# Four graph layers on one core: relational loops over tiles ordered by node block, second relation table and output made inside the loops

## The chip, the cores and the metric

The kernel runs on one core of one Trainium2 chip. The metric is device time in microseconds of one execution. Before the change it is 18669.26 us, the median of three runs (18641.42 to 18669.32).

## The reference, cut to what matters

Four layers over 12500 nodes and 212500 edges sorted by destination: a weighted sum over edges, a hyperbolic layer, three attention layers, and two relational layers, each added to `x`. The change rewrites the last layer:

```python
def _rgcn_conv(x, src, dst, edge_type, W_r, W_root, b):
    seg = dst * r + edge_type
    agg = segment_sum(x[src], seg).reshape(n, r, d)
    mean = agg / maximum(cnt, 1.0)
    return einsum('nrd,rdk->nk', mean, W_r) + x @ W_root + b
h = x                              # 12500 x 64
for l in range(2):                 # 65 relations, W[l] is 65 x 64 x 64
    h = relu(_rgcn_conv(h, ..., W[l], root[l], bias[l])) + relu(h @ res_W[l] + res_b[l])
```

## The kernel before, in words

Engines run their own streams and meet at counting semaphores; a `Phase` (L165) owns its buffers and semaphores and ends with a barrier of all engines. Edges stand in 1664 tiles of 128 (`ET`), in chunks of `K` = 8 tiles: 208 chunks. Nodes stand in blocks of 128.

The order of phases (L2462 to L2520) is: `prepare` (edge arrays padded, loaded and transposed), `begin` (x loaded, layer norm), `project`, `bucket_places` (a histogram loop), `edges_ordered` (edges scattered by source into a DRAM bucket of 65 MB, which `prepare` clears with 48 DMAs on ACT's queue, L285), the first two layers, three attention layers with `after_attention`, and then twice this:

- `typed_tables` (L2085): for 100 node blocks, 9 products give h times each of 65 relation matrices and of `root` and `res_W` (67 rows of 64 floats a node). PE makes them, ACT and DVE copy them out of PSUM, SP stores 2.1 MB a block to the DRAM table `typed`.
- `edges_relational` (L2190): per chunk, POOL gathers 8 x 128 rows of the table by source and relation (L2231). DVE scales them by 1/count (L2303) and makes a one-hot of the place of each edge in its tile's window (`member`, L2275). PE multiplies both (`product`, L2361), and DVE adds the 64 x 128 result into `sums`, a column per node, at a register's offset (L2320). The first relational loop also finds 1/count: SP loads 8 windows of `inv_count` a chunk (L2220), PE transposes `member` (L2343), ACT copies that out (L2255), PE multiplies it with the window (`from_dst`, L2351), DVE picks the relation (L2280, L2288, L2293).
- `columns_to_nodes` (L1625) transposes `sums`, and `after_relational` (L2382) adds the own rows and biases.

`rounds` (L128) writes each engine's order out by hand: a list of (step, lead), where turn t does the step of chunk t + lead, four turns to a loop body. Buffers have 2 or 4 slots, so a step waits for the chunk 2 or 4 before it.

## Time and profile before

| | us |
|---|---|
| median of three runs | 18669.26 |
| profiled execution, its own time | 18656.17 |
| its span | 18654.4 |
| PE, DVE, ACT, POOL busy | 12203.1, 12936.0, 7253.8, 11319.3 |

The span is cut into stages by phase. Times below are from the span's start. A row of the timeline gives start, duration, engine, line, operation with its tiles, how many are merged, and in brackets the idle time before it and what ended it. No engine is busy for more than 69% of the span, so what a stage costs is read from the wait that ends last in it.

### The profile page before, as it was taken

To read this page: it belongs to the slowest core of one execution; us is meant where nothing else is said; L and a number is where in the kernel's file an instruction comes from. 1 tells how busy PE (TensorE), PEld (TensorE's weight loads), DVE (VectorE), ACT (ScalarE), POOL (GpSimd) and SP (SyncE) were. 2 spreads that over 40 slices of the span, in tenths; PEclk is the share of its full clock that TensorE was granted. 3 is DMA by queue.
4 is the path that set the end of the run, shared out by engine and by line. 5 is a ranking of instruction groups with operands and counts; after the bars stand their busy time and mean duration, and the time that the engine had idled before them with its cause. 6 is when DMAs were issued, how large, how long until landed. Compare 5 with 4: busy or idle time off the path is not lost. (4 is left out here: it accounts for less than half of the span.)

```text
span 18654.4 us, 354278 instructions
## 1 busy us (share of the span) xinstructions
PE 12203.1 (65%) x79434; PEld 9406.9 (50%) x79435; DVE 12936.0 (69%) x30593; ACT 7253.8 (39%) x19156; POOL 11319.3 (61%) x11773
## 2 busy tenths in 40 slices
PE   3434436499996577776777767777777776843333
PEld 2322224366664466664666656665456665533332
DVE  4877768777776788887888878887555555543334
ACT  0111118455554466654666546665321111410000
POOL 0477770177774477774777657776047776057775
PEclk9999999977776565555655555565886666965555
DMA  5233334333334222223222222223752223931112
GB/s 190 69 94 94 94 86 111 93 103 102 103 102 81 59 58 58 58 54 57 58 58 58 57 54 58 58 58 62 325 188 53 53 53 59 375 118 26 26 26 47
DMA packets 1461776, 1649.61 MB, mean 88 GB/s; under 512 B 964011, under 2 KB 1068475, under 8 KB 1429565
## 3 DMA queue, kind: packets, MB, share of 16 engines
q1 hardware_dynamic: 1050273, 1054.17, 19.2%
q0 software_dynamic: 404480, 528.97, 14.4%
q10 hardware_dynamic: 6912, 65.18, 0.8%
q8 instruction: 46, 0.75, 0.0%
q14 instruction: 65, 0.53, 0.0%
HBM read 1028.36 MB, written 623.09 MB: 89 GB/s over the span
## 5 line engine op out<-in xcount | busy, mean ns | idle before, releaser
L1791 POOL DMA_INDIRECT gat_from_src<-gat_src_dram,gat_src_at x4992 | 4813.9, 964 | 2261.2 <-issue 1520.4
L2231 POOL DMA_INDIRECT rel_from_src<-typed_dram,rel_src_at x3328 | 3168.3, 952 | 2386.1 <-ACT rel_src_at L2245 1374.4
L2361 PE MATMUL rel_ps_sum<-all_node,rel_msg 128*64 128x128 f32 x6656 | 1518.8, 404 | 1667.6 <-DVEq L2323 1638.4
L1337 POOL DMA_INDIRECT all_node<-hyp_dst_dram,hyp_src_at x1768 | 1716.3, 971 | 1419.8 <-ACT hyp_src_at L1355 900.2
L2008 PE MATMUL gat_ps_sum<-all_node,gat_msg 128*80 128x128 f32 x9984 | 2267.7, 420 | 42.3 <-DVE gat_msg L1904 7.6
L2361 PEld LDWEIGHTS rel_ps_sum<-all_node,rel_msg 128*64 128x64 f32 x6656 | 1214.7, 211 | 1920.1 <-DVEq L2323 1490.9
L2008 PEld LDWEIGHTS gat_ps_sum<-all_node,gat_msg 128*80 128x80 f32 x9984 | 2057.5, 252 | 102.6 <-issue 43.0
L839 POOL DMA_INDIRECT bucket_dram<-all_node,order_index x1664 | 1614.4, 970 | 531.3 <-issue 506.4
L1952 DVE TENSOR_TENSOR gat_sums<-gat_sums,gat_ps_sum 80x128 f32 x4992 | 1390.5, 279 | 380.9 <-DVE gat_sums L1952 212.4
L1914 DVE TENSOR_TENSOR_SCAN gat_ps_log<-gat_masks,gat_top,gat_ps_log 8x1024 f32<-8x1024 bf16 x624 | 1461.8, 2343 | 227.1 <-DVE gat_sums L1952 218.4
L1986 PE MATMUL gat_ps_log<-all_ident,gat_leaky 128*8 128x128 f32 x4992 | 1072.0, 388 | 719.8 <-DVE gat_leaky L1899 719.8
L1821 ACT ACTIVATE gat_off<-all_iota,gat_edge 128x128 bf16<-128x128 bf16 x4992 | 1516.0, 386 | 0.2 <-issue 0.2
L1921 DVE TENSOR_TENSOR_SCAN gat_top<-gat_masks,gat_ps_log 8x1024 f32<-8x1024 bf16 x624 | 1419.2, 2274 | 35.0
L2320 DVE TENSOR_TENSOR rel_sums<-rel_sums,rel_ps_sum 64x128 f32 x3328 | 918.6, 276 | 688.9 <-issue 506.9
L1977 PE MATMUL gat_ps_dst<-again_gat_here,gat_memberT 128*128 x9984 | 1124.4, 197 | 81.3 <-ACT gat_memberT L1841 69.9
L1977 PEld LDWEIGHTS gat_ps_dst<-again_gat_here,gat_memberT 128*128 128x128 bf16 x9984 | 967.2, 108 | 366.5 <-issue 126.8
L984 PE MATMUL order_ps_dst<-all_node 128*128 128x64 bf16 x4992 | 300.6, 240 | 1225.5 <-ACT all_node L864 1152.5
L1851 ACT ACTIVATE gat_shift<-gat_shift 8x1 f32<-8x1 f32 x624 | 126.4, 203 | 2363.7 <-DVE gat_shift L1928 2363.7
L1986 PEld LDWEIGHTS gat_ps_log<-all_ident,gat_leaky 128*8 128x8 f32 x4992 | 509.4, 112 | 1034.9 <-DVE gat_leaky L1899 648.6
L2185 PE MATMUL typed_bank<-typed_w,typed_ft 64*128 64x512 f32 x3600 | 902.0, 585 | 109.2 <-ACT typed_res L2146 89.7
L2255 ACT ACTIVATE all_node<-rel_ps_turn 128x512 f32<-128x512 f32 x416 | 225.8, 594 | 1811.6 <-PE rel_ps_turn L2343 1793.0
L1995 PE MATMUL gat_ps_top<-all_ident,gat_top 8*128 8x8 f32 x4992 | 503.4, 224 | 631.8 <-DVE gat_shift L1928 631.8
(450 smaller groups left out, 26609.9 us busy)
## 6 DMA issues: line engine op xcount, KB each, us to landing
typed_dram<-typed_res SPq DMA_DIRECT2D x200, 2144.0 KB
gat_relrow<-in_rows_dram SPq DMA_DIRECT2D x624, 256.0 KB
all_node<-gcn_table_dram SPq DMA_DIRECT2D x1664, 48.0 KB
gat_from_src<-gat_src_dram,gat_src_at POOLq DMA_INDIRECT x4992
bucket_dram<-by_dst_zero ACTq DMA_DIRECT2D x48, 1326.0 KB
gsum_rec<-bucket_dram SPq DMA_DIRECT2D x221, 288.0 KB, 2.8
all_node<-lo_rows_dram SPq DMA_DIRECT2D x221, 256.0 KB
rel_table<-inv_count_dram SPq DMA_DIRECT2D x1664, 32.5 KB
```

What stands on the lines that cost most here:

```text
L839: nc.gpsimd.indirect_dma_start(g.bucket[:, :], bass.IndirectOffsetOnAxis(ap=index[:, q, k:k + 1], axis=0), rec[:, q, k, :], None).then_inc ...
L1337: nc.gpsimd.indirect_dma_start(from_dst[:, q, k, :], None, g.hyp_dst[:, :], bass.IndirectOffsetOnAxis(ap=src_at[:, q, k:k + 1], axis=0)).t ...
L1791: nc.gpsimd.indirect_dma_start(from_src[:, q, k, :], None, g.gat_src[:, :], bass.IndirectOffsetOnAxis(ap=src_at[:, q, k:k + 1], axis=0)).t ...
L1821: last = nc.scalar.activation(off[:, k, :], g.iota16[:, :], ACT.Abs, scale=-1.0, bias=edge[:, q, REL, k:k + 1])
L1914: v.tensor_tensor_scan(log_flat, masks[:, q, 0, :], log_flat, top[:, 1 - q % 2, CE - 1:CE], ALU.add, ALU.max).then_inc(step_b, 1)
L1921: v.tensor_tensor_scan(top[:, q % 2, ::-1], masks[:, q, 1, ::-1], log_flat[:, ::-1], -BIG, ALU.add, ALU.max).then_inc(step_b, 1)
L1952: v.tensor_tensor(window, window, ps_sum[0:rows, k, :], ALU.add).then_inc(step_c, 1)
L1977: last = nc.tensor.matmul(dst_v[:, k, :], memberT[:, q % 2, w, k, :], own[:, w, :, :].rearrange("p n h -> p (n h)"), start=w == 0, stop=w ...
L1986: last = nc.tensor.transpose(ps_log[0:H, k, :], leaky[:, q % 2, k, :], g.ident[:, :])
L2008: last = nc.tensor.matmul(ps_sum[0:rows, k, :], msg[:, q % 2, k, :], member[:, q, k, :], start=True, stop=True)
L2231: nc.gpsimd.indirect_dma_start(from_src[:, q, k, :], None, g.typed[:, :], bass.IndirectOffsetOnAxis(ap=src_at[:, q, k:k + 1], axis=0)).the ...
L2361: last = nc.tensor.matmul(ps_sum[0:D, k, :], msg[:, q % 2, k, :], member[:, q, k, :], start=True, stop=True)
```

## The change

1. **Order of tiles.** In `prepare` and a new phase `tile_order` a place is computed for every edge tile, such that all tiles that add into a node block have been processed at a fixed turn: block j of a computed order is complete after chunk 2j + 16. Tile rows (source times 65 plus relation, place, relation, base) are scattered to DRAM by 26 indirect DMAs on POOL in `bucket_places`, and read and transposed in the last `after_attention`.
2. **A second list of steps.** `slotted` runs steps of chunks as `rounds` does, and steps of a block on every other turn.
3. **First relational loop.** After block j is complete: PE multiplies its 128 columns with `mix` (identity, root and residual), ACT adds biases and takes relu, PE folds the halves, ACT keeps the result, PE makes the 65 products, ACT copies them, and SP stores 2.08 MB into `typed_next`. The transposition of `member` on PE and its copy on ACT go; SP loads each chunk's places broadcast to 128 partitions (`relrow`, 256 KB) and DVE compares them with the lane (`turned_ones`).
4. **Second relational loop.** Per block, one PE product with `mix`, ACT relu, one PE product, one DVE add into `x`, which is stored at the end.
5. **Gone:** the second `typed_tables`, both `columns_to_nodes` of the relational layers, both `after_relational`, and `typed_index`. The first table has 98 blocks of 65 rows a node instead of 100 of 67.
6. **Start.** x is loaded in `prepare`, after the edge arrays. The 48 clears go on POOL's queue, two in flight: 8 in `prepare` after x has landed, 10 in `begin`, 30 in `bucket_places`.

```diff
+def slotted(eng, steps, count=CHUNKS, slots=OWN_TILES):
+    def turn(t, i, q, late):
+        for step, lead, *off in steps:
+            if not off:
+                    step(t + lead, (q + lead) % 4, i + (q + lead) // 4)
+            elif late and (q - off[0]) % 2 == 0:
+                h = (q - off[0]) // 2
+                    step(i * 2 + h, h % 2, i + h // 2)
+def clear_buckets(nc, g, pool, first, last):
+    for n in range(first, last):
+        if n >= 2:
+            pool.wait_ge(g.zeroed[n % 2], 16 * (n // 2))
+        nc.gpsimd.dma_start(rows[:, n * ZERO:(n + 1) * ZERO], g.zero[:, :]).then_inc(g.zeroed[n % 2], 16)
...
 def prepare(nc, g):
+                pool.wait_ge(padded, 7)
+                pool.wait_ge(rows_in, 7 * 16)
+                pool.wait_ge(x_in, 32)
+                clear_buckets(nc, g, pool, 0, 8)
...
-                for n in range(CLEARS):
-                    act.dma_start(flat[:, n * ZERO:(n + 1) * ZERO], g.zero[:, :]).then_inc(g.zeroed, 16)
...
 def edges_relational (SP)
                     def load(c, q, i):
                         sp.wait_ge(inverse, free2(c))
+                        sp.dma_start(relrow[:, q % 2, :], g.tile_rels...[ds(c * CE, CE)]
+                                     .partition_broadcast(P)).then_inc(rel_in[q], 16)
                         for k, b in enumerate(bases(nc, ENG.SP, g.base, c)):
-                            sp.dma_start(table[:, q % 2, k, :], g.inv_count[ds(b, P), :]).then_inc(win[q], 16)
-                    rounds(sp, [(load, 0)])
+                            sp.dma_start(table_in[:, q % 2, k, :], g.inv_count[ds(b, P), :]).then_inc(win[q], 16)
+                    def store(j, s, m):
+                        sp.wait_ge(copied, (j + 1) * len(groups) + 2)
+                        at = place_of(ENG.SP, j, g.order_at, NB * P - P)
+                        sp.dma_start(next_rows[ds(at, P), :], res[:, s, :]).then_inc(put[s], 16)
+                    slotted(sp, [(load, 2), (store, None, LAG + 4)])
...
 (ACT)
-                rounds(act, [(fields, 4)] + ([(turn_out, 3)] if first else []))
+                    slotted(act, [(fields, 4), (activate, None, LAG), (keep, None, LAG + 1),
+                                  (copies(groups[0:5]), None, LAG + 2), (copies(groups[5:9]), None, LAG + 3)])
...
 (DVE)
+                def turned_ones(c, q, i):
+                    dve.wait_ge(rel_in[q], 16 * (i + 1))
+                    dve.wait_ge(inverse, free2(c))
+                    v.tensor_scalar(memberT[:, q % 2].rearrange("p k e -> p (k e)"), relrow[:, q % 2, :], g.lane[:, 0:1],
+                                    None, ALU.is_equal).then_inc(turned, 1)
...
-                                 (choose, 2), (add(3), 0), (take, 2), (add(4), 0), (zero_ones, 3), (add(5), 0),
-                                 (keep, 2), (add(6), 0), (add(7), 0)])
+                                 (choose, 2), (add(3), 0), (take, 2), (add(4), 0), (zero_ones, 3), (turned_ones, 3),
+                                 (add(5), 0), (keep, 2), (add(6), 0), (add(7), 0)])
...
 (PE)
+                def products(part):
+                            pe.wait_ge(copied, j * len(groups) + q + 1)
+                            nc.tensor.matmul(banks[(len(groups) * s + q) % 2][:, 0:n * D], ft[lane, s, :],
+                                             w[lane, o:o + n * D], start=True, stop=True).then_inc(made, 1)
-                    rounds(pe, [(from_dst, 2), (product(0), 1), (turn_members, 3), (product(1), 1)])
+                    slotted(pe, [(from_dst, 2), (mix_node, None, LAG), (fold_node, None, LAG + 1),
+                                 (products(groups[0:2]), None, LAG + 2), (products(groups[5:7]), None, LAG + 3),
+                                 (product(0), 1),
+                                 (products(groups[2:4]), None, LAG + 2), (products(groups[7:9]), None, LAG + 3),
+                                 (product(1), 1), (products(groups[4:5]), None, LAG + 2)])
```

PE in the first relational loop. Before, one turn of the loop is (`rel_ps_sum` is `product`, `rel_ps_turn` the transposed `member`, `rel_ps_inv` is `from_dst`):

```order
L2351 MATMUL rel_ps_inv<-rel_table,all_node 128x65 x8
L2359 ISA
L2361 MATMUL rel_ps_sum<-all_node,rel_msg 64x128 x4
L2340 REGISTER_ALU
L2343 MATMUL rel_ps_turn<-all_ident,all_node 128x128 x8
L2361 MATMUL rel_ps_sum<-all_node,rel_msg 64x128 x4
```

After the change the odd turn of that loop, in which the last products of a block stand (`rel_bank`), is:

```order
L2653 MATMUL rel_ps_inv<-rel_table_in,all_node 128x65 x8
L2680 REGISTER_ALU
L2683 MATMUL rel_ps_node<-rel_act_x,rel_fold 128x128
L2697 REGISTER_ALU
L2699 MATMUL rel_bank<-rel_w,rel_ft 128x512
L2697 REGISTER_ALU
L2699 MATMUL rel_bank<-rel_w,rel_ft 128x512
L2661 ISA
L2663 MATMUL rel_ps_sum<-all_node,rel_msg 64x128 x4
L2697 REGISTER_ALU
L2699 MATMUL rel_bank<-rel_w,rel_ft 128x512
L2697 REGISTER_ALU
L2699 MATMUL rel_bank<-rel_w,rel_ft 128x64
```

The eight transposes have left, and a fold and four products of a block stand around the first half of the chunk's own product; the second half, L2663 again, follows them.

SP in the same loop, after the change, from the end of one chunk's windows to the start of the next chunk's:

```order
L2466 DMA rel_table_in<-inv_count_dram 128x65
L183 TENSOR_LOAD all_order_at
L2471 ISA
L2471 DMA typed_next_dram<-rel_res 128x4160
L2463 DMA rel_relrow<-tile_rels_dram 128x1024
L183 TENSOR_LOAD again_base
L2466 ISA
```

Before, this stream held window loads alone. Now the store of a block stands ahead of the next chunk's places and windows, on the same queue, every other chunk.

## Rows read from the trace of the kernel before

**Rows 1.** Windows: clears, histogram, typed tables, first relational loop, second.

```profile
core 0: us, PE busy (x) PEld busy (x) DVE busy (x) ACT busy (x) POOL busy (x), PEclk, DMA share, GB/s
5.00:200.00 195.00, 0.00 (x0) 0.00 (x0) 4.79 (x5) 0.00 (x0) 0.00 (x0) 1.00 0.96 383
356.00:576.00 220.00, 169.80 (x1656) 153.24 (x1656) 195.38 (x208) 36.61 (x206) 1.60 (x1) 1.00 0.00 0
...
13200.00:13600.00 400.00, 359.09 (x1436) 220.94 (x1433) 208.20 (x375) 196.46 (x450) 0.00 (x0) 1.00 0.98 414
14446.00:14912.00 466.00, 355.87 (x1865) 304.87 (x1863) 261.05 (x646) 61.06 (x188) 352.94 (x372) 0.68 0.29 53
17242.00:17708.00 466.00, 181.71 (x744) 145.79 (x744) 186.07 (x467) 21.19 (x141) 352.79 (x372) 0.50 0.15 26
```

**Rows 2.** Timeline of the start: first cast, begin, project.

```profile
195.07 5.27 DVE L299 CAST prep_rows<-prep_raw 128x1664 f32<-128x1664 int32 x5 [191.05 <-DMA prep_raw<-weight_padded_dram]
...
245.73 0.22 DVE L420 MEMSET begin_x<- 128x192 f32 x1 [1.46 <-PEq L178]
...
263.59 6.82 DVE L386 TENSOR_REDUCE begin_stat<-begin_x 128x100 f32<-128x6400 f32 x1 [17.64 <-DMA begin_x<-in_x]
...
305.89 1.17 SPq L497 DMA_DIRECT2D gcn_in_w<-in_L_gnn_kernel  x2
```

**Rows 3.** Groups by shape, first relational loop: busy, mean ns, idle before.

```profile
L2231 POOL DMA_INDIRECT rel_from_src<-typed_dram,rel_src_at x797 | 758.6, 952 | 242.9 <-issue 242.9
...
L2303 DVE TENSOR_TENSOR rel_msg<-rel_from_src,rel_inv 128x512 f32<-128x512 f32 x99 | 69.2, 699 | 242.8 <-DMA rel_from_src<-typed_dram,rel_src_at 242.8
```

**Rows 4.** Timeline between the two relational loops.

```profile
15798.27 0.69 DVE L2303 TENSOR_TENSOR rel_msg<-rel_from_src,rel_inv 128x512 f32<-128x512 f32 x1 [6.04 <-DMA rel_from_src<-typed_dram,rel_src_at]
...
16436.99 0.95 POOL L2231 DMA_INDIRECT rel_from_src<-typed_dram,rel_src_at  x1 [642.15 <-ACT rel_src_at L2245]
```

**Rows 5.** Timeline of the end.

```profile
18538.69 0.70 PEld L1637 LDWEIGHTS rel_ps_inv<-all_ident,rel_sums 64*128 64x128 f32 x8 [2.97 <-issue]
...
18636.93 0.41 SPq L2401 DMA_DIRECT2D out<-rel_end_x  x1
```

**Rows 6.** Window of begin's load of x.

```profile
246.00:262.00 16.00, 0.00 (x0) 0.00 (x0) 0.00 (x0) 0.50 (x1) 0.00 (x0) 1.00 0.99 193
```

**Rows 7.** DMA issues of the page: KB each, us to landing.

```profile
gsum_rec<-bucket_dram SPq DMA_DIRECT2D x221, 288.0 KB, 2.8
```

**Rows 8.** Timeline, typed tables: PE at half clock, ACT's copy, SP's stores.

```profile
15895.63 6.45 PE L2185 MATMUL typed_bank<-typed_w,typed_ft 64*128 64x512 f32 x18
...
15897.74 0.60 ACT L2146 ACTIVATE typed_res<-typed_bank 128x512 f32<-128x512 f32 x1 [2.29 <-PE typed_bank L2185]
...
16395.19 32.29 SPq L2128 DMA_DIRECT2D typed_dram<-typed_res  x7
```

**Rows 9.** DMA queues, first relational loop: packets, MB, share of 16 engines.

```profile
q0 software_dynamic: 11872, 12.18, 14.6%
```

**Rows 10.** Timeline of the first relational loop, PE, DVE and SP.

```profile
14993.86 3.95 SPq L2220 DMA_DIRECT2D rel_table<-inv_count_dram  x8
...
15000.83 3.68 PE L2351 MATMUL rel_ps_inv<-rel_table,all_node 128*128 128x65 f32 x16
...
15008.19 0.69 DVE L2320 TENSOR_TENSOR rel_sums<-rel_sums,rel_ps_sum 64x128 f32 x2
...
15009.78 1.09 PE L2361 MATMUL rel_ps_sum<-all_node,rel_msg 128*64 128x128 f32 x8
...
15011.19 1.99 PE L2351 MATMUL rel_ps_inv<-rel_table,all_node 128*128 128x65 f32 x16 [0.33 <-issue]
...
15019.15 1.97 PE L2361 MATMUL rel_ps_sum<-all_node,rel_msg 128*64 128x128 f32 x8
```

**Rows 11.** Groups by shape, second attention layer.

```profile
L1791 POOL DMA_INDIRECT gat_from_src<-gat_src_dram,gat_src_at x631 | 608.4, 964 | 192.3 <-issue 192.3
...
L1871 DVE TENSOR_SCALAR gat_memberT<-gat_relrow,all_lane 128x1024 bf16<-128x1024 bf16 x79 | 37.6, 476 | 0.0
```

More of the change, by code:

```diff
@@ L52 @@
 SORTS = 5
-SIDX, INV = range(2)
+SIDX, INV = SRC, END
+ROW = 3 * P + 4
+LAG = 16
 class Chain:
@@ L2043, in _ @@
                     sp.wait_ge(stored, 16)
+            if last:
+                @block.tensor
+                def _(pe):
+                    pe.wait_ge(row_in, 16)
+                    for n, (f, b, m) in enumerate(pieces):
+                        if n >= 2:
+                            pe.wait_ge(rows_c, n - 1)
+                        wide = P if f < 3 else 1
+                        for k in range(m):
+                            turned = nc.tensor.transpose(turn[n % 2][0:wide, k * P:(k + 1) * P],
+                                                         tile_row[:, b + k, f * P:f * P + wide], g.ident[:, :])
+                        turned.then_inc(rows_t, 1)
             @block.scalar
@@ L2209, in edges_relational @@
[L2209 to L2216 removed]
+        inv = ph.sb("inv", [P, 2, K])
+        mix, fold, bias_col, lower = (ph.sb("mix", [P, P]), ph.sb("fold", [P, P]), ph.sb("bias_col", [P, 1]),
+                                      ph.sb("lower", [P, 1]))
@@ new lines, in place_of, with _ @@
+        def place_of(engine, j, order, top):
+            (reg,) = bases(nc, engine, order, j, count=1, per=1, top=top)
+            return reg
+        with nc.Block() as block:
+            @block.sync
+            def _(sp):
+                if first:
+                    prime(sp, ph, g, put)
+                sp.dma_start(mix[D:P, 0:D], root).then_inc(w_in, 16)
+                sp.dma_start(mix[D:P, D:P], res_w).then_inc(w_in, 16)
+                sp.dma_start(bias_col[0:D, :], bias.unsqueeze(1)).then_inc(w_in, 16)
+                sp.dma_start(bias_col[D:P, :], res_bias.unsqueeze(1)).then_inc(w_in, 16)
+                if first:
+                    load_relations(sp, w, relations, w_in)
@@ new lines, in copies, with step @@
+                def copies(part):
+                    def step(j, s, m):
+                        for q, r, n, _, _ in part:
+                            if q == 0:
+                                act.wait_ge(put[s], 16 * m + 16)
+                                alone(act, mark_a)
+                            act.wait_ge(made, (j + 2) * len(groups) + q + 1)
+                            nc.scalar.activation(res[:, s, r * D:(r + n) * D], banks[(len(groups) * s + q) % 2][:, 0:n * D],
+                                                 ACT.Copy).then_inc(copied, 1)
+                    return step
@@ L2364, in product @@
                     return step
-                if first:
-                    rounds(pe, [(from_dst, 2), (product(0), 1), (turn_members, 3), (product(1), 1)])
-                else:
-                    rounds(pe, [(product(0), 1), (product(1), 1)])
-        turn = [ps_inv[:, n, :] for n in range(2)]
-        columns_to_nodes(nc, g, ph, sums, D, turn)
-def typed_index(nc, g):
-    with nc.Block() as block:
-        @block.vector
-        def _(dve):
-            nc.vector.scalar_tensor_tensor(g.typed_at[:, SIDX, :], g.edges[:, SRC, :], float(RT), g.edges[:, TYPE, :],
-                                           ALU.mult, ALU.add)
```

499 lines of the change are left out of this document (347 added, 152 removed).

## The prediction, made before the changed kernel had run

> **What bounds the kernel now.** I read the page's slices first, then windows over each stage, the groups by shape inside the relational loop, the waits, and the timeline at the joints between stages. The change touches four stretches, and each has its own bound.
>
> The start is DMA. From 5 to 200 us the DMA engines are busy for 96% of the time at 383 GB/s and no engine computes [rows 1]. That is the clearing of the bucket, and the first cast waits 191.05 us for the edge arrays queued beside it, until 195.07 [rows 2].
>
> The typed tables are DMA too: share 0.98 at 414 GB/s, PE busy 359.09 of 400 us at full clock [rows 1].
>
> The relational loops are POOL. Its gathers stand 372 to 466 us in both loops [rows 1]: 1.255 us each, of which 0.952 is the instruction and 0.30 the gap behind it (242.9 us over 797) [rows 3]. Eight make a chunk, 10.04 us, and 208 chunks 2088 us. DVE waits 2.45 us of each chunk for them (242.8 over 99) [rows 3], so the first loop has some slack, the second more (PE busy 181.71 of 466) [rows 1].
>
> The joints are serial: 642.15 us without a gather between the loops [rows 4], and 116 us from the last gather's use to the end of the span (18654.4) [rows 5].
>
> **The change part by part**, against the profiled execution (18656.17 us, 13 us under the median).
>
> *Start.* Without the clears ahead of them, the edge arrays have 4.2 MB of copies and 6.0 MB of loads to wait for. At 414 GB/s that is 25 us, at 193 GB/s, the rate of x's own load [rows 6], 53 us; three landings of some 2 us (2.8 less the transfer of 288 KB [rows 7]) and issue add 8. Between 33 and 61 I take 48, so the cast starts 147 us earlier. Loading x inside `prepare` hides the 17.64 us wait in `begin` [rows 2]: -18. Added in `prepare`: eight small DVE steps of 0.2 us and four long ones, of 1664 elements at the 1.07 ns an element that 6400 in 6.82 us show [rows 2], partly at twice that speed: +8. `tile_order` is new: 2548 elements and four passes of 1274, 8 us; some 35 small steps, 9; 26 tiny products at the histogram's 0.10 us (169.80 over 1656) [rows 1], 3; five round trips and a barrier, 6: +26, between 18 and 35. The clears move under other work: 65 MB at 414 GB/s is 3.3 us each. Eight (27 us) lie under `prepare`'s 50 us of compute, ten (33 us, beside the store of x) under `begin`'s 42 us (305.89 - 263.59 [rows 2]), thirty (99 us) and 26 scatters (33 us) on POOL under the histogram loop, where DMA stands at 0.00 for 220 us [rows 1]. If that cover failed they would cost up to 40 us. I count 1. Sum: -147 - 18 + 8 + 26 + 1 = **-130**.
>
> *First typed tables.* A store took 5.23 us from issue to issue (32.29 less an issue, over 6 intervals and a bit; 2.14 MB at 414 GB/s is 5.2) [rows 8]. 98 blocks of 65 rows for 100 of 67 leaves 497 of 523 us: **-26**. DVE's extra copy of 0.3 us a block lies under the store.
>
> *Between the loops.* The 642 us become: the last gather's landing and use (9 us, to 15803), then the tail of three blocks, because block j's products stand four turns behind its last chunk. Nine copies of 0.60 us on ACT, each paired with a product through two banks, and mix, fold and keep make some 11 us a block: 33. Then the last store with its landing, 7, a barrier, 3, and the first copies, 6, since ACT now waits for eight small DVE steps: 58 in all. **-584**, give or take 15.
>
> *End.* From 18538.69 the old end needs 98 us to the store of `out` at 18636.93 [rows 5]; the new one two blocks of mix, relu, product and add, 3.5 us each: **-91**. The store itself stays.
>
> *Second loop.* PE gets two products per two chunks (1 us of 20), DVE one add. Covered by POOL: 0.
>
> *First loop.* Work first. PE loses the transposes (2 us a chunk) and gains, per two chunks, nine products of 0.49 us at full clock (359.09 x 5.23/400 a block, less a transpose) or 0.72 and more at half [rows 1, 8], mix and fold. ACT loses 1.2 and gains 3 us a chunk, DVE gains about 0.65. None passes 10 us at full clock. The wait is elsewhere: `store` stands on SP ahead of the next chunk's `relrow` and windows, and waits for copies that need late products of PE's odd turn. That closes a ring of two chunks. From product 7 of a block: products 7 and 8 with copy, 2.0; SP's register load and issue, 1.1; start and landing of a DMA 2.1 [rows 7]; the block's store ahead of it, 2.13 MB at 414 GB/s, 5.1, stretched by the gathers' 14.6% of the DMA engines to 5.9 [rows 9]; `relrow` 0.6: 11.7. Then DVE: `turned_ones` 0.7 and three adds (two take 0.69) with `keep`, 1.5: 13.9. PE's second half product of that turn waits for these adds: 1.09 at full or 1.97 at half clock, product 4 0.9 or 1.7, `from_dst` of the next chunk 1.99 or 3.68 [rows 10], fold 0.5 or 0.8, products 5 and 6 1.0 or 1.7, first half product 1.1 or 2.0. The ring is **20.5 us at full clock and 25.8 at half**, against 20.08 for sixteen gathers. PE idles about a third of it and the granted clock was 0.68 at 76% busy, 0.50 at 39% [rows 1], so after each idle stretch it would start at 1.2 GHz (0.50) and rise: with the first of these six at half the ring takes 21.4, with the first two 22.2. I take 21.8, as the loop was granted more than half clock at a similar load: +1.7 us on each of 94 pairs of chunks, **+160**. Bounds of the drain: 5.1 us, what this same store took [rows 8], up to 11.0, were it to run at x's 193 GB/s [rows 6]. The windows' eight issues (3.95 us [rows 10]) go on under the drain.
>
> The Trainium skill, page DMA: Bandwidth & Descriptors, section Queues, rings and completion order, says that descriptors of one queue are consumed in ring order on each DMA engine; by that the places wait behind the whole store, as in the ring. If they did not, the ring would lose 5.9 us and the loop stay on POOL's pace: 160 us less.
>
> POOL's rate could fall, too. In the attention layers, where DVE does this comparison in bf16 (0.476 us), a gather takes 964 ns and not 952 [rows 11]: 0.1 us a chunk, 20 us if POOL is the bound, nothing while the ring is. The Trainium skill, page SBUF — State Buffer, section Who interferes with whom, states that a DVE operation in a two-port mode locks GpSimd out of the shared port for its whole length. A full block of 0.65 us a chunk would be up to 135 us; the attention row speaks for far less.
>
> Barriers and the rest: **+8**. Sum: -130 - 26 - 584 - 91 + 160 + 8 = -663. 18656 - 663 = **17993 us**.
>
> **The rivals.**
> *A: the ring hides.* If PE stays at full clock the ring (20.5) is POOL's pace. The gathers run up to four chunks ahead, which absorbs jitter. For it: PE at 1.00 with 90% busy in the tables; against: idle stretches of several us. Then -823, and 0.4 us a pair at most: 17833 to 17873. 30%.
> *B: the drain is slow.* At 8 to 9 us, half way to x's rate, because 16.6 KB rows meet the gathers' 256-byte rows: another 2.4 us a pair: 18220. 12%.
> *C: PE at half clock throughout.* The granted clock was 0.50 in the second loop [rows 1], where PE idles more than half. 25.8 us a pair, +538 in place of +160: 18371. 9%.
> *D: slower than before.* Without the loop's term the sum is -823; the change loses from 28.8 us a pair of chunks on (20.08 + 823/94). The place is the same ring: the drain would have to take 14 us at full clock, or 9 at half clock. At half clock with the drain at 193 GB/s the pair takes 30.9 us: +1017 - 823, 18850. Both ends must meet; 2%.
> *E: the start gains nothing*, the edge arrays being bound by their small packets and not by the clears: then cast stays near 195 and the sum is 147 higher, 18140. The 96% share of the clears speaks against it; 3%.
>
> **How the numbers follow.** My forecast has 44%. The predicted time is its own, 17993. Its own error is 70 us: 15 in the tail, 20 at the start, 60 for one step of the clock. The range takes in A and B with their errors and leaves out C, D and most of what lies below A: **17815 to 18300**. A change of 0.2% (37 us) is about what a measurement of this kernel can tell from none. Faster by more: all but D and a little: 0.97; same 0.01; slower 0.02.
>
> **What would show it.** The first cast near 48 us and `gcn_in_w` near 175 us. No typed tables after the first loop, and some 60 us without a gather. The end 20 to 30 us behind the last message. In the first loop gathers at 10.9 us a chunk, with DVE waiting for `relrow` in every other turn and SP's store at the head of that wait; if A is right, POOL's gaps stay 0.30 us and DVE waits for gathers only. Granted clock 0.65 to 0.85 there. The forecast is wrong if the first loop's pace is outside 10.0 to 12 us a chunk, or if the clears come up in the waits of `edges_ordered`.

## The result, and the profile after

The changed kernel takes 18149.09 us (median of 4 runs, 18136.91 to 18195.42), the kernel before 18666.64 beside it: ratio 0.973, 95% interval 0.9711 to 0.9749. The profiled execution has a span of 18151.6 us against 18654.4: **502.8 us less**. The forecast was 17993, 663 us less, with 17815 to 18300 as its range. The sign and the range held; 160 us of the gain did not come.

The start, two timelines of the changed kernel (start us, duration, engine, line, operation; in brackets the idle time before and what ended it):

```profile
46.02 5.27 DVE L347 CAST prep_raw<-prep_raw 128x1664 f32<-128x1664 int32 x5 [41.79 <-DMA all_node<-weight_padded_dram]
...
170.29 1.22 SPq L651 DMA_DIRECT2D gcn_in_w<-in_L_gnn_kernel  x2
```

The first cast starts at 46.02 instead of 195.07, `gcn_in_w` is loaded at 170.29 instead of 305.89 [rows 2]. The forecast had 48 and about 175.

The joints of the last part: where the typed tables begin and end, the two loops, the end of the program (timelines of the changed kernel):

```profile
13054.25 4.78 SPq L2325 DMA_DIRECT2D typed_dram<-typed_res  x2
...
13565.19 0.96 POOL L2491 DMA_INDIRECT rel_from_src<-typed_dram,rel_src_at  x1 [518.96 <-ACT rel_src_at L2506]
...
15953.28 0.95 POOL L2491 DMA_INDIRECT rel_from_src<-typed_dram,rel_src_at  x1 [0.30 <-issue]
...
16026.85 0.95 POOL L2491 DMA_INDIRECT rel_from_src<-typed_next_dram,rel_src_at  x1 [72.62 <-ACT rel_src_at L2506]
...
18118.97 0.95 POOL L2491 DMA_INDIRECT rel_from_src<-typed_next_dram,rel_src_at  x1 [0.30 <-issue]
...
18133.85 0.42 SPq L2478 DMA_DIRECT2D out<-rel_x  x1
```

There is no typed table after the first loop any more: the gap without a gather is 72.62 us where 642.15 stood [rows 4]. `out` is stored 15 us behind the last gather. But the first loop lasts from 13565.2 to 15953.3, **2388 us**, where the same 1664 gathers took 2091 before (13702.9 to 15793.9).

Windows over the changed kernel: the bucket stage, the sums after it, the first relational loop before its first table block is ready, in its middle and late, and the second loop:

```profile
core 0: us, PE busy (x) PEld busy (x) DVE busy (x) ACT busy (x) POOL busy (x), PEclk, DMA share, GB/s
503.00:2623.00 2120.00, 845.07 (x7428) 513.71 (x7428) 1622.92 (x4759) 413.95 (x2056) 1613.25 (x1663) 0.50 0.35 94
2760.00:3250.00 490.00, 395.98 (x5008) 280.50 (x5008) 468.13 (x1203) 470.32 (x1404) 0.00 (x0) 0.50 0.43 121
13620.00:13780.00 160.00, 110.81 (x472) 97.40 (x472) 94.52 (x225) 4.76 (x29) 122.73 (x122) 0.50 0.36 75
14446.00:14912.00 466.00, 366.72 (x1610) 242.50 (x1609) 235.20 (x558) 110.12 (x299) 296.41 (x300) 0.72 0.52 148
15500.00:15800.00 300.00, 270.40 (x1273) 183.08 (x1272) 187.29 (x444) 89.03 (x240) 230.78 (x228) 0.77 0.63 179
16500.00:16966.00 466.00, 211.32 (x831) 167.92 (x832) 189.58 (x487) 21.25 (x117) 353.10 (x371) 0.50 0.14 26
```

From 14446 to 14912, the window of [rows 1], 300 gathers start instead of 372. The second loop keeps 371.

The groups of that window (busy us, mean ns, idle before, what ended it):

```profile
L2491 POOL DMA_INDIRECT rel_from_src<-typed_dram,rel_src_at x300 | 297.2, 991 | 171.6 <-ACT rel_src_at L2506 85.9 <-issue 85.7
L2699 PE MATMUL rel_bank<-rel_w,rel_ft 64*128 64x512 f32 x296 | 147.1, 842 | 0.0
L2573 DVE TENSOR_SCALAR all_node<-rel_relrow,all_lane 128x1024 f32<-128x1024 bf16 x37 | 28.3, 764 | 63.0 <-DMA rel_relrow<-tile_rels_dram 63.0
L2587 DVE TENSOR_TENSOR rel_kinds<-rel_kinds,rel_ps_inv 128x520 f32<-128x520 f32 x38 | 26.4, 693 | 101.7 <-PE rel_ps_inv L2653 101.7
```

Against [rows 3] two things are new. POOL waits 85.9 us for ACT's copy of the gather indices. That copy waits for no buffer: ACT stands still only before its other instructions, 243.2 us of it before the copies of a block's products, until PE has made them, and the index copy of the next chunk stands behind these in ACT's list. So something ahead of PE's products is late. And its gathers themselves take 991 ns in the mean, not 952.

The timeline shows what is late. First a slow turn, then one late in the loop (PE, DVE's comparison and SP, and one gather):

```profile
14432.86 0.35 SPq L2471 DMA_DIRECT2D typed_next_dram<-rel_res  x1
14433.47 0.33 SPq L2463 DMA_DIRECT2D rel_relrow<-tile_rels_dram  x1
...
14441.65 0.81 DVE L2573 TENSOR_SCALAR all_node<-rel_relrow,all_lane 128x1024 f32<-128x1024 bf16 x1 [3.80 <-DMA rel_relrow<-tile_rels_dram]
...
14443.79 1.94 PE L2663 MATMUL rel_ps_sum<-all_node,rel_msg 128*64 128x128 f32 x8 [5.68 <-DVEq L2622]
...
14447.66 3.68 PE L2653 MATMUL rel_ps_inv<-rel_table_in,all_node 128*128 128x65 f32 x16
...
14449.26 0.95 POOL L2491 DMA_INDIRECT rel_from_src<-typed_dram,rel_src_at  x1 [5.32 <-ACT rel_src_at L2506]
...
14457.74 0.36 SPq L2471 DMA_DIRECT2D typed_next_dram<-rel_res  x1
```

```profile
15617.97 0.35 SPq L2471 DMA_DIRECT2D typed_next_dram<-rel_res  x1
15618.50 1.66 PE L2663 MATMUL rel_ps_sum<-all_node,rel_msg 128*64 128x128 f32 x8 [1.84 <-DVEq L2622]
...
15620.09 3.68 PE L2653 MATMUL rel_ps_inv<-rel_table_in,all_node 128*128 128x65 f32 x16
...
15627.11 0.75 DVE L2573 TENSOR_SCALAR all_node<-rel_relrow,all_lane 128x1024 f32<-128x1024 bf16 x1
...
15629.63 1.09 PE L2663 MATMUL rel_ps_sum<-all_node,rel_msg 128*64 128x128 f32 x8
...
15638.42 0.36 SPq L2471 DMA_DIRECT2D typed_next_dram<-rel_res  x1
```

In the slow turn `relrow` is issued 0.6 us behind the store and is there 8.2 us later; DVE waits 3.80 us for it, PE 5.68 us for DVE's adds, and comes back at half clock (1.94 us for eight products, 3.68 for `from_dst`). The block's copies are late by that, the next store too, and the turn takes 24.9 us from store to store. In the other turn DVE does not wait for `relrow`, PE's longest wait for DVE is 1.84 us, and the turn takes 20.5. The loop is in one or the other way of running: of 103 intervals of sixteen gathers 50 are over 23 us (nearly all of these 24 to 26.7) and the others mostly 20.3 to 21.6.

The fast turn has its half clock too: its first `from_dst` takes 3.68 us. What differs is where it falls. Windows over the two turns, each from the store to the comparison that needs the places behind it, and from there to the next store (the number before the last two is the granted clock):

```profile
14432.86:14441.65 8.79, 5.25 (x33) 3.37 (x32) 4.10 (x10) 2.54 (x5) 6.73 (x7) 0.97 0.93 310
14441.65:14457.74 16.09, 13.81 (x54) 9.15 (x54) 8.16 (x22) 3.35 (x11) 8.55 (x9) 0.59 0.31 61
15617.97:15627.11 9.14, 8.61 (x34) 6.58 (x35) 5.04 (x11) 1.14 (x3) 7.00 (x8) 0.55 0.91 301
15627.11:15638.42 11.31, 9.99 (x54) 6.08 (x52) 7.59 (x20) 4.84 (x14) 8.87 (x9) 0.91 0.41 85
```

In the fast turn the half clock lies under the store's drain, where the time is taken anyway. In the slow one it lies behind the comparison, on the work that the next store waits for. The same holds over the loop. Of the 93 turns from store to store in which a comparison follows the store (all but the last four), 35 are under 23 us and 58 over. The first part takes 9.1 us in the mean of either kind. The second takes 10.9 us at a granted clock of 0.96 in the fast ones, and 16.3 us at 0.59 in the slow ones. The clock of the whole turn hardly tells them apart: 0.79 and 0.72.

### The profile page after: what moved, and what is told of

It reads as the page before. It is cut to its first block and busy times, and to the rows that moved or that the text cites. A ratio compares the mean times of both kernels' runs of the same rounds, so it can differ in the third digit from the quotient of the medians.

```text
span 18151.6 us, 353694 instructions
## 1 busy us (share of the span) xinstructions
PE 12184.2 (67%) x78268; PEld 9151.3 (50%) x78269; DVE 12774.8 (70%) x30479; ACT 7296.9 (40%) x19211; POOL 11490.6 (63%) x11850
## 3 DMA queue, kind: packets, MB, share of 16 engines
q1 hardware_dynamic: 1055441, 1076.43, 20.3%
## 5 line engine op out<-in xcount | busy, mean ns | idle before, releaser
L2663 PE MATMUL rel_ps_sum<-all_node,rel_msg 128*64 128x128 f32 x6656 | 1421.1, 384 | 1632.7 <-DVEq L2622 1541.0
L2491 POOL DMA_INDIRECT rel_from_src<-typed_dram,rel_src_at x1664 | 1667.2, 1002 | 1240.8 <-ACT rel_src_at L2506 760.6
L2663 PEld LDWEIGHTS rel_ps_sum<-all_node,rel_msg 128*64 128x64 f32 x6656 | 1137.9, 199 | 2137.4 <-DVEq L2622 1186.5
L2491 POOL DMA_INDIRECT rel_from_src<-typed_next_dram,rel_src_at x1664 | 1585.9, 953 | 579.8 <-issue 492.6
L2619 DVE TENSOR_TENSOR again_sums_x<-again_sums_x,rel_ps_sum 64x128 f32 x3328 | 917.8, 276 | 691.5 <-issue 400.2
L2141 PE MATMUL gat_ps_dst<-gats_gat_here,gat_memberT 128*128 x9984 | 1132.8, 197 | 82.9 <-ACT gat_memberT L2005 70.1
L2141 PEld LDWEIGHTS gat_ps_dst<-gats_gat_here,gat_memberT 128*128 128x128 bf16 x9984 | 969.0, 108 | 376.5 <-issue 136.0
L1148 PEld LDWEIGHTS order_ps_dst<-all_node 128*128 128x128 bf16 x4992 | 271.7, 129 | 1271.7 <-issue 922.5
```

The costliest lines, as they stand in the source:

```text
L2141: last = nc.tensor.matmul(dst_v[:, k, :], memberT[:, q % 2, w, k, :], own[:, w, :, :].rearrange("p n h -> p (n h)"), start=w == 0, stop=w ...
L2491: nc.gpsimd.indirect_dma_start(from_src[:, q, k, :], None, table[:, :], bass.IndirectOffsetOnAxis(ap=src_at[:, q, k:k + 1], axis=0)).then_ ...
L2663: last = nc.tensor.matmul(ps_sum[0:D, k, :], msg[:, q % 2, k, :], member[:, q, k, :], start=True, stop=True)
```

## The experiments

All are edits of the changed kernel, and the profile of each was read in the same window.

**1. The store moved to ACT's queue.** SP is left with the loads.

```
-                    slotted(sp, [(load, 2), (store, None, LAG + 4)])
+                    rounds(sp, [(load, 2)])
...
+                def store(j, s, m):
+                    at = place_of(ENG.Activation, j, g.order_at, NB * P - P)
+                    act.wait_ge(copied, (j + 1) * len(groups) + 2)
+                    nc.scalar.dma_start(next_rows[ds(at, P), :], res[:, s, :]).then_inc(put[s], 16)
```

> One edit: the block's store is issued from ACT's queue, behind ACT's last copy, and no longer from SP ahead of the next chunk's relrow. In the changed kernel a pair of chunks of the first relational loop takes either 19.5 to 20.5 us or 24 to 26 us. Theory 1 (the ring through the store): with the store out of SP's queue DVE no longer waits for relrow, PE is idle less and keeps its full clock, and the pair goes to 20 to 21 us nearly everywhere: first loop 2389 -> 2120 to 2180 us, kernel about 17900. Theory 2 (PE's half clock alone, whatever the store does): the loop stays within 60 us of 2389, kernel 18090 to 18180. Theory 3 (the store's traffic slows relrow and the gathers on the DMA engines, whichever queue it is in): DVE's waits for relrow stay near 3.5 us in every other turn, loop 2350 to 2400.

Measured: 17934.89 us (2 runs, 17929.32 to 17940.46). First loop 2185 us, no interval over 23 us, the pair 21.0. DVE no longer waits for `relrow`:

```profile
L2487 POOL DMA_INDIRECT rel_from_src<-typed_dram,rel_src_at x357 | 357.4, 1001 | 108.9 <-issue 106.1 <-DVE rel_msg L2604 1.5 <-ACT rel_src_at L2502 1.2
...
L2575 DVE TENSOR_SCALAR all_node<-rel_relrow,all_lane 128x1024 f32<-128x1024 bf16 x44 | 32.4, 737 | 0.0
```

The ring went through the store on SP: theory 1. Theory 3 falls, since the same bytes go at the same time (176 GB/s in the window). The Trainium skill, page DMA: Bandwidth & Descriptors, section Queues, rings and completion order, has descriptors of one queue consumed in ring order on each DMA engine; the trace agrees, with `relrow` landing 8.2 us after issue behind the store and DVE not waiting for it once it is alone with the windows. That it is not quite POOL's old pace (20.1) has another cause: POOL's gaps are 0.30 us again, and the gathers are long.

**2. PE given work where it idles.** Eight products a chunk into PSUM columns that nobody reads.

```
+                def warm(c, q, i):
+                    for k in range(8):
+                        nc.tensor.matmul(ps_inv[:, k % 2, 4 * R:4 * R + P], g.ident[:, :], g.iota[:, :],
+                                         start=True, stop=True)
...
-                                 (product(1), 1), (products(groups[4:5]), None, LAG + 2)])
+                                 (warm, 0), (product(1), 1), (products(groups[4:5]), None, LAG + 2)])
```

> One edit: PE gets eight more products a chunk in the first relational loop (float32, 128x128, 0.27 us each at full clock, as many as the transposes that the change took out), into PSUM columns that nobody reads, just ahead of the second half product, where PE stands idle. The result is unchanged. Theory 1 (PE's clock falls for want of work): the granted clock of the loop rises above 0.9, the slow pairs of 24 to 26 us go, the first twenty chunks go from 10.8 to 10.4 us each, first loop 2389 -> 2120 to 2200 us. Theory 2 (the clock is not what matters, the ring is long by itself): PE's added 2.2 us (4.4 at half clock) a chunk come on top, loop 2450 to 2800 us.

Measured: 17947.44 us (17941.99 to 17952.89). First loop 2195 us, one interval over 23 us. With the store where it was, and more work on PE, the slow intervals are gone:

```profile
14446.00:14912.00 466.00, 410.96 (x2559) 298.43 (x2558) 273.66 (x652) 127.69 (x345) 358.10 (x355) 0.94 0.62 175
...
L2573 DVE TENSOR_SCALAR all_node<-rel_relrow,all_lane 128x1024 f32<-128x1024 bf16 x44 | 33.1, 753 | 32.3 <-DMA rel_relrow<-tile_rels_dram 32.3
```

Granted clock 0.94 for 0.72. DVE still waits for `relrow`, 0.73 us a chunk instead of 1.70 (63.0 over 37), but POOL's buffers cover that. So the slow turn needs both: the store in the way, and PE at half clock behind the comparison. Of the 93 turns from store to store 65 now take 19.8 us in the mean and are granted 1.00 in both parts. The other 28 still take 24.8, but come one or two at a time, where the changed kernel had up to sixteen in a row, and the gathers, four chunks ahead, ride over them.

**3. Another form of DVE's comparison.** Both sources stay in SBUF.

```
-                    v.tensor_scalar(memberT[:, q % 2].rearrange("p k e -> p (k e)"), relrow[:, q % 2, :], g.lane[:, 0:1],
-                                    None, ALU.is_equal).then_inc(turned, 1)
+                    v.tensor_tensor(memberT[:, q % 2].rearrange("p k e -> p (k e)"), relrow[:, q % 2, :],
+                                    g.lane[:, 0:1].broadcast_to([P, CE]), ALU.is_equal).then_inc(turned, 1)
```

> One edit: DVE's comparison that makes memberT from relrow is a tensor_tensor against the broadcast lane instead of a tensor_scalar: 1.2 us in place of 0.73. In the changed kernel the gathers beside that comparison take 1.2 to 1.47 us and not 0.95 (mean 1002 ns over the first loop, 952 in the second). Theory 1 (DVE's short form holds POOL up, and only where POOL is the bound does it cost): the gathers' mean falls to about 955 ns; the loop has 0.5 us a chunk more in the ring of DVE and PE, and loses it where the ring binds: first loop 2389 -> 2390 to 2460 us. Theory 2 (POOL held up is what costs the 137 us that the forecast missed): first loop 2300 to 2320 us. Theory 3 (the long gathers come from the DMA traffic of the store): the mean stays near 1000 ns.

Measured: 18291.02 us (two runs, 157 us apart: 18212.37 and 18369.67), first loop 2448 us, inside theory 1's range, but for another reason. All three missed on the gathers: their mean neither fell nor stayed, it rose.

```profile
L2491 POOL DMA_INDIRECT rel_from_src<-typed_dram,rel_src_at x327 | 337.3, 1032 | 128.8 <-issue 94.5 <-ACT rel_src_at L2506 34.0 <-DVE rel_msg L2602 0.3
...
L2573 DVE TENSOR_TENSOR all_node<-rel_relrow,all_lane 128x1024 f32<-128x1024 bf16 x41 | 49.8, 1215 | 38.3 <-DMA rel_relrow<-tile_rels_dram 38.1
```

The longer DVE's comparison, the longer the gathers beside it: it is the comparison that holds POOL up, but not by its short form.

**4. The clears first, as before.** All 48 are issued on ACT's queue at the start of `prepare`, and POOL's three groups of clears are taken out.

```
+            @block.scalar
+            def _(act):
+                act.wait_ge(padded, 7)
+                flat = g.bucket.rearrange("(p w) f -> p (w f)", p=P)
+                for n in range(CLEARS):
+                    act.dma_start(flat[:, n * ZERO:(n + 1) * ZERO], g.zero[:, :]).then_inc(g.zeroed[n % 2], 16)
```

> One edit: the 48 clears of the bucket go back to ACT's queue at the very start, as in the kernel before; all else is the changed kernel. Theory 1 (the edge arrays stood behind the clears): the first cast goes from 46 to about 190 us and everything behind it shifts by 140 to 150 us: first scatter of the bucket from 503 to about 640 us, kernel 18285. Theory 2 (the arrays are bound by their own small packets): the first cast stays below 70 us and the kernel within 20 us of the changed one.

Measured: 18290.05 us (18238.06 to 18342.03). The start is back where it was:

```profile
194.72 5.27 DVE L353 CAST prep_raw<-prep_raw 128x1664 f32<-128x1664 int32 x5 [190.49 <-DMA all_node<-weight_padded_dram]
...
646.67 1.04 POOL L1009 DMA_INDIRECT bucket_dram<-all_node,order_index  x1 [24.07 <-ACT all_node L1034]
```

The first scatter of the bucket comes 144 us later than in the changed kernel (503). Theory 1 holds, and rival E of the forecast falls. The span of the profiled execution is only 85 us longer, because it had 36 slow intervals instead of 50 and a first loop of 2331 us: the first sign that their number is not fixed. The median is 141 us longer.

**5. The lane number read from PSUM**, on top of experiment 1.

```
-        iota = ph.ps("ps_iota", [P, 512])[:, 0:P]
+        ps_const = ph.ps("ps_iota", [P, 512])
+        iota, lane_ps = ps_const[:, 0:P], ps_const[:, P:P + 1]
...
-                    v.tensor_scalar(memberT[:, q % 2].rearrange("p k e -> p (k e)"), relrow[:, q % 2, :], g.lane[:, 0:1],
-                                    None, ALU.is_equal).then_inc(turned, 1)
+                    v.tensor_tensor(memberT[:, q % 2].rearrange("p k e -> p (k e)"), relrow[:, q % 2, :],
+                                    lane_ps.broadcast_to([P, CE]), ALU.is_equal).then_inc(turned, 1)
```

> On top of the kernel with the store on ACT's queue (21.0 us a pair of chunks everywhere, 10.5 a chunk): memberT's comparison reads the lane number from PSUM, in a tensor_tensor of 1.2 us in place of the 0.73 us tensor_scalar, so that only one of its two sources lies in SBUF. In the run where it was the same tensor_tensor with both sources in SBUF, the gathers beside it were longer still (mean 1036 ns). Theory 1 (POOL is held up by a DVE operation that reads and writes SBUF alone, and that is the floor of 21.0): the gathers' mean falls from 1006 to 960 to 970 ns, the pair to 20.2 to 20.5 us, first loop 2185 -> 2105 to 2140 us, kernel 17860 to 17890. Theory 2 (any DVE operation of that place and length holds POOL up, wherever its sources lie): the mean stays at 1006 ns or rises to 1036, loop 2185 to 2240. Theory 3 (0.5 us a chunk more on DVE binds, since PE and DVE wait for each other): gathers short, but the pair at 21 to 22 us.

Measured: 17908.31 us (17897.54 to 17919.08), first loop 2179 us, the median interval 20.54 us, the mean 20.24 over the first twenty chunks, where no block is made yet (20.89 in experiment 1), two intervals over 23.

```profile
L2488 POOL DMA_INDIRECT rel_from_src<-typed_dram,rel_src_at x356 | 341.9, 961 | 125.5 <-issue 105.2 <-ACT rel_src_at L2503 20.3
...
L2577 DVE TENSOR_TENSOR all_node<-rel_relrow,rel_ps_iota 128x1024 f32<-128x1024 bf16 x44 | 52.9, 1202 | 0.0
```

The same operation, as long as in experiment 3 and in the same place, no longer holds POOL up: 961 ns for 1032. Two things differ from experiment 3, the place of the second source and the store's queue. The queue is not it: with the store on ACT's queue alone the gathers took 1001 ns, and with the source in PSUM and the store left on SP (experiment 10) they take 960. Theory 1 is right on the gathers, theory 3 on why the loop gained only 6 us: PE is granted 0.79, and POOL waits 20.3 us for index copies that stand in ACT's list behind late copies of products.

**6. Store on ACT's queue and the added products together.**

> Both edits that each took the slow pairs away: store on ACT's queue, and eight more products a chunk on PE. Theory 1 (each edit alone already brings the loop to POOL's pace, which is 16 gathers with their gaps, 20.08 us, and 0.9 us in which POOL is held up): together they bring nothing more: pair 21.0 us, first loop 2175 to 2200 us, kernel 17930. Theory 2 (each leaves some slow turns of its own behind, and these make the 0.9 us): pair 20.1 to 20.5 us, first loop 2100 to 2130.

Measured: 17922.73 us (17920.19 to 17925.27), first loop 2177 us, mean interval 20.94 us, mean gather 1005 ns. Theory 1: with either cure alone the first loop is within 20 us of both together, and most of what is left over POOL's old pace is POOL held up.

**7. memberT made by ACT**, on top of experiment 1.

```
+                def far_distances(c, q, i):
+                    act.wait_ge(rel_in[q], 16 * (i + 1))
...
+                    nc.scalar.activation(far_d[:, :], relrow[:, q % 2, :], ACT.Abs, scale=-1.0, bias=g.lane[:, 0:1]
+                                         ).then_inc(far_off, 1)
...
+                    nc.scalar.activation(memberT[:, q % 2].rearrange("p k e -> p (k e)"), far_d[:, :], ACT.Relu,
+                                         scale=-1.0, bias=1.0).then_inc(turned, 1)
```

> On top of the kernel with the store on ACT's queue: memberT is made by ACT in two passes (distance, then 1 minus it cut at 0), and DVE has no comparison with relrow at all. Theory 1 (DVE's comparison is what holds POOL up): the gathers' mean falls from 1006 to 955 to 970 ns and the pair to 20.1 to 20.5 us if ACT's two passes of about 1 us are early enough: first loop 2100 to 2140 us. Theory 2 (ACT becomes late: its copies of the products stand behind the two passes, and the passes behind the wait for relrow): pair 21.5 to 24 us, with PE waiting for ACT's copies. Theory 3 (POOL is held up by the traffic of the store and not by DVE): mean stays near 1006 ns.

Measured: 18402.81 us (18399.91 to 18405.7), first loop 2640 us, 90 intervals over 23 us. The gathers are short (969 ns), as theory 1 has it, and the loop is slow, as theory 2 has it: PE waits for ACT's passes (102.9 us over 36 chunks of the window at `from_dst`).

**8. Store, added products and lane in PSUM.** Experiments 1, 2 and 5 together; then timed again over five rounds.

> Store on ACT's queue, eight more products a chunk on PE, lane in PSUM. If the clock is what makes DVE's extra 0.5 us a chunk matter (PE at half clock between DVE's adds), the added products help here: pair 20.1 to 20.4 us, first loop 2095 to 2125 us, kernel 17840 to 17880, 10 to 60 us below the one without them. If POOL's pace is all that is left, the two are within 15 us of each other.

> Store on ACT's queue, eight more products a chunk, lane in PSUM, timed against the changed kernel. With no slow pairs left there is nothing left to chance: times within 20 us of 17862, 1.5 to 2% below the changed kernel.

Measured: 17861.73 us, and 17860.94 again (5 runs, 17848.88 to 17865.25), first loop 2122 and 2119 us. Against experiment 5 the added products bring 47 us: with PE near full clock (0.98) DVE's longer comparison no longer costs.

**9. The changed kernel again.**

> The changed kernel once more, beside the best variant on the same chip. If which turns fall to half clock is a matter of chance from run to run, its times spread over some 100 us (18130 to 18250) and the count of slow pairs in the profile differs from the 50 of the first profile, with a pair at either 19.5 to 21 or 24 to 26 us again; if the pattern is fixed by the program, the profile shows 50 again within two or three, and the times lie within 30 us.

Measured: 18088.61 us (6 runs, 18019.41 to 18210.1), 34 slow intervals in the profiled run and a first loop of 2321 us. The kernel before had 18647.14 to 18656.02 over 11 runs on the same chip. The changed kernel's ten runs are spread over 190 us (18019 to 18210), the two runs each of experiments 3 and 4, which kept both kinds of turns, over 157 and 104. Those of experiments 1, 2, 5, 6, 8 and 10 are within 4 to 22 us. Experiment 7, slow from the first blocks to the end, is within 6. How many turns run slow is chance from execution to execution, and a gain against this kernel is known only as well as that.

**10. Added products and lane in PSUM, the store left on SP.** Two edits, 2 and the comparison of 5.

> The changed kernel with its store where it was, on SP ahead of relrow, with eight more products a chunk and the lane in PSUM. Theory 1 (the ring through the store is no longer than POOL's pace as long as PE keeps its full clock): DVE still waits for relrow in every other turn, but the pair takes 20.1 to 20.6 us, first loop 2110 to 2150 us, within 30 us of the variant with the store on ACT's queue. Theory 2 (with DVE's 0.5 us a chunk more in it the ring is over POOL's pace even at full clock, 20.5 + 0.5 to 1.0): pair 21.0 to 21.6 us, first loop 2180 to 2250.

Measured: 17845.15 us (17839.61 to 17850.69), ratio to before 0.9568 (0.9551 to 0.9584), first loop 2108 us, mean interval 20.28: the best of all.

```profile
14446.00:14912.00 466.00, 412.46 (x2706) 299.85 (x2706) 310.61 (x687) 136.18 (x368) 353.82 (x369) 0.99 0.64 183
...
L2492 POOL DMA_INDIRECT rel_from_src<-typed_dram,rel_src_at x369 | 354.4, 960 | 112.5 <-issue 105.8 <-ACT rel_src_at L2507 5.2 <-DVE rel_msg L2604 1.5
...
L2575 DVE TENSOR_TENSOR all_node<-rel_relrow,rel_ps_iota 128x1024 f32<-128x1024 bf16 x46 | 55.7, 1211 | 14.6 <-DMA rel_relrow<-tile_rels_dram 14.3
```

Theory 1: at full clock the ring through the store, with the 5 us of its drain and DVE's longer comparison in it, is within POOL's pace. 369 gathers start in the window, 372 before the change.

## Why the forecast held, and where it was off

By the marks of the two profiled executions:

| term | forecast | measured | from |
|---|---|---|---|
| start | -130 | -137 | first scatter of the bucket 639.88 -> 502.7 |
| barriers and the rest, up to the typed tables | +8 | +22 | first store of a typed table 13168.9 -> 13054.2, less the start |
| typed tables | -26 | -23 | first store to first gather, 534.0 -> 511.0 |
| first loop | +160 | +297 | first to last gather, 2091 -> 2388 |
| between the loops | -584 | -570 | last to first gather, 643.1 -> 73.6 |
| second loop | 0 | +3 | 2089 -> 2092 |
| end | -91 | -96 | last gather to the end of the span, 128.4 -> 32.6 |
| sum | -663 | -503 | |

**Start.** Right in mechanism and size; experiment 4 shows that it was the clears (144 us). They came up in no wait of the bucket stage: first to last scatter 2120 us before and after.

**Typed tables, end, second loop.** Right within 5 us each.

**Between the loops.** 14 us too little, within the 15 given. It varies with how the first loop ends: 48.6 us in experiment 1, 58.5 in experiment 9.

**First loop: right in the ring, wrong in its clock.** The ring is the one described: product, copy, store, `relrow`, comparison, adds, product. The drain was sized right: 8.2 us from the issue of `relrow` to its use in the slow turn, for the 8.6 that were set (2.1, 5.9 and 0.6), so rival B was not it. Its two lengths were nearly right as well: 20.5 with the six pieces of PE work behind the comparison at full clock and 25.8 with them at half, measured 20.0 and 25.3 from store to store (means of the fast and of the slow turns). The step that failed is the mix: "with the first of these six at half the ring takes 21.4, with the first two 22.2. I take 21.8". There is no such mean. The half clock does not take the first one or two of the six pieces; it covers most of them (granted 0.59) or hardly any (0.96). In the slow turn shown, PE waits 5.68 us for DVE, the clock falls in that wait (granted 1.00 up to 14441.2 us, 0.50 from there to 14454.9), and the work behind it runs at half clock and makes the next store late, so that the next turn is like it. In the fast turn PE is at half clock under the drain and back at full clock soon behind the comparison (granted 0.91 from there to the store). That each turn passes its kind on in this way is read from the order of events; experiment 2, which fills PE's idle place and takes the slow turns away, bears it out. What moves the loop from one kind to the other is open. It stays in either for several turns, slow for up to sixteen from store to store, and ran slow in 50 of 103 intervals, each some 4 us over the others: about 195 us, where rival C (half clock throughout) had 9% and 538 us, and rival A (no cost) 30%.

**First loop, second part: POOL's rate.** The forecast saw that DVE's comparison could slow the gathers, took the attention layers' 964 ns as the price, and wrote "0.1 us a chunk, 20 us if POOL is the bound, nothing while the ring is", with "up to 135 us" as the far end. Measured: 0.45 us a chunk in experiment 1, where POOL has its gaps of 0.30 us again (21.0 us a pair for 20.1), which over 208 chunks is 94 us. Experiment 10 differs from experiment 2 in the comparison alone, and its loop is 87 us shorter. Not all of it is the comparison: the gathers of experiment 5 are still 0.06 us a chunk over the old 953 ns (the last section has the rest). The attention row was the wrong neighbour: it has bf16 on both sides and takes 0.476 us, this one writes float32 in 0.74. 195 and 94 make the 297 within 8.

**What was luck.** The range held with 150 us to spare at its upper end, but that end was set for rival B, the slow drain, and the drain was not slow; what filled it were the mix of turns and POOL's rate. And the size of the miss is itself in part chance: in the second profile of the same kernel the first loop took 2321 us and not 2388.

The Trainium skill, page SBUF — State Buffer, section Who interferes with whom, says that DVE in a two-port mode takes the ports it shares with GpSimd for its whole length, and that an operation with at most one SBUF input outside those modes takes none. Experiment 5 agrees with the second (961 ns); whether the comparison of the changed kernel runs in a two-port mode, no run here shows. The same section says that an instruction of DVE with two SBUF inputs contends with one of GpSimd that reads SBUF, and infers that it leaves the making of descriptors alone. The gathers read their indices from SBUF, and experiment 3 agrees with the first (1032 ns) and differs from the inference; the measurement decides.

**The rest up to the typed tables.** 14 us above the 8 forecast. Of the 22, 12.6 lie in the sums behind the bucket stage: 539.9 us from first to last load for 527.3, and the same 540 in every profile of the changed kernel and its variants. The same instructions run there with the same durations. The granted clock differs: 1.00 in this stage before, 0.50 in all the others, and DVE waits 21.9 us for PE's sums in a window of 490 us where it waited 12.5. Against the clock as the cause stands that the kernel before took 18651.2 and 18656.0 us in its two runs at a mean clock of 0.71, and 18647 to 18655 in the nine at 0.62 (experiment 9). No run sets the clock of that stage alone, and the cause stays open.

## What to carry to other kernels

When a step that keeps TensorE busy is taken out of a loop, look at what its idle stretches do to its clock, and compute a ring of waits at both clock levels as two ways of running, not as a mean: ask on which part of the ring the slow stretch will lie, since the mean clock of a turn did not show it here (0.79 and 0.72). If the slow way makes its own idle time, the loop stays in it. Useless products in an idle place took 141 to 202 us away here (17947 against the two medians of the changed kernel, 18089 and 18149). Next to a loop bound by indirect DMAs on POOL, check each DVE operation that has all its operands in SBUF, and where the gathers begin beside it; one source in PSUM was enough to free POOL, even in an operation 0.5 us longer.

## What the runs showed of the hardware that was not expected

- The granted clock depends on what went before. In the bucket stage the same instructions at the same 845 us of PE work in 2120 were granted 1.00 in the profiled execution before and 0.50 after; PE had fallen to 0.50 at about 80 us, in `prepare`, and rose again only behind the sums that follow the bucket stage. It cost nothing there: the stage takes 2120 us either way. Of the 11 runs of the kernel before beside experiment 9 two had a mean clock of 0.71 and nine 0.62, at times of 18647 to 18656 us. The fall of the mean clock from 0.707 to 0.613 is therefore mostly no sign of the change.
- Gathers beside a DVE operation with all its operands in SBUF get longer. Over the whole first loop they took 1029 ns in the mean beside the `tensor_tensor` comparison of 1.2 us (experiment 3), 1009 beside the `tensor_scalar` of 0.74 us (experiment 1), and 961 beside the same `tensor_tensor` with one source in PSUM (experiment 5), for 953 before the change.
- What decides is where the gather begins, and `messages`, a `tensor_tensor` of 0.7 us with both sources in SBUF, shows it. It stood in the loop before, too, where it did no harm. A pair from experiment 10, one from before, and one of the `tensor_scalar` from experiment 1:

```profile
15654.71 0.68 DVE L2604 TENSOR_TENSOR rel_msg<-rel_from_src,rel_inv 128x512 f32<-128x512 f32 x1
15655.02 1.20 POOL L2492 DMA_INDIRECT rel_from_src<-typed_dram,rel_src_at  x1 [0.30 <-issue]
...
15002.16 0.95 POOL L2231 DMA_INDIRECT rel_from_src<-typed_dram,rel_src_at  x1 [0.30 <-issue]
15002.23 0.69 DVE L2303 TENSOR_TENSOR rel_msg<-rel_from_src,rel_inv 128x512 f32<-128x512 f32 x1 [2.85 <-DMA rel_from_src<-typed_dram,rel_src_at]
...
15661.73 1.29 POOL L2487 DMA_INDIRECT rel_from_src<-typed_dram,rel_src_at  x1 [0.31 <-issue]
...
15662.17 0.73 DVE L2575 TENSOR_SCALAR all_node<-rel_relrow,all_lane 128x1024 f32<-128x1024 bf16 x1
```

  In experiment 10, 82 gathers begin inside `messages`, between 0.05 us behind its start and 0.15 us ahead of its end. Each of them ends 0.82 to 0.83 us behind it, and so takes 1.00 to 1.46 us. One more begins 0.02 us ahead of it and takes 1.52; no other gather of that loop takes over 0.98. In the kernel before only three begin inside, and they end 0.82 to 0.83 us behind it as well: there `messages` waited for the landing of a gather and mostly began just behind the start of a later one. That is the 0.06 to 0.15 us a chunk left in experiments 5, 7, 8 and 10. The comparison of experiment 3 does the same to the 173 gathers that begin inside it (0.82 to 0.83 us behind its end). With one source in PSUM, in experiment 5, 192 begin inside it and take 0.95 to 0.96 us all the same. The `tensor_scalar` holds up gathers that began ahead of it, too, as in the last pair. What in the two operations makes that difference is open.
